# Channel weights prepared in one row behind the first pair's mix, their large transfers issued later

## The reference, cut to what matters

```python
x = x + conv(_ln_c(x))            # relation-aware attention over space, then over channels
t = tokens(x)
t = t + moe(_ln_t(t))             # router over 8 experts, top 2, 128x128 weights per expert
```

```python
theta_c = relu(bn(thc_w @ xc)); phi_c = relu(bn(phc_w @ xc)); g = relu(bn(gxc_w @ xc))   # each (196, 784)
```

## Time and profile before

| | before |
|---|---|
| median of 3 runs | 1772.88 us |
| profiled execution | 1769.24 us |
| its span | 1767.4 us |
| TensorE busy | 1681.3 us (95%) |
| VectorE busy | 1432.0 us (81%) |
| ScalarE busy | 1180.4 us (67%) |
| GpSimd busy | 1110.7 us (63%) |
| mean granted TensorE clock | 0.991 |
| HBM traffic | 106.50 MB read, 26.13 MB written |

### The profile page before, as it was taken

One profiled execution on the slowest core, in us unless ns is written; L12 is line 12 of the kernel. 1 busy time (PEld: TensorE's weight loads), 2 busy tenths in 40 slices (PEclk: granted clock), 3 DMA queues, 4 the chain that ended last, 5 costly groups with the idle time before them and its releaser, 6 DMA issues.

```text
span 1767.4 us, 38965 instructions
## 1 busy us (share of the span) xinstructions
PE 1681.3 (95%) x13140; PEld 1281.1 (72%) x13140; DVE 1432.0 (81%) x4704; ACT 1180.4 (67%) x3346; POOL 1110.7 (63%) x1268
## 2 busy tenths in 40 slices
PE   4789999999999999999999999999999999999985
PEld 3567777777777777777777777777777777777673
DVE  4557888888888888888888888888888888888766
ACT  3557666667766767776676776666677667677543
POOL 1245666676666777666667666666766667675555
PEclk9899999999999999999999999999999999999998
DMA  5122222111222211222221122221112222111110
GB/s 140 37 75 74 76 90 93 71 69 66 93 74 93 93 56 68 81 93 74 93 87 53 65 92 76 91 93 68 72 66 93 74 93 92 56 66 65 56 56 37
DMA packets 56179, 135.15 MB, mean 76 GB/s; under 512 B 16268, under 2 KB 18333, under 8 KB 55982
## 3 DMA queue, kind: packets, MB, share of 16 engines
q1 hardware_dynamic: 55320, 130.81, 21.2%
q10 hardware_dynamic: 662, 1.84, 0.4%
HBM read 106.50 MB, written 26.13 MB: 75 GB/s over the span
## 4 chain that ended last, share of the span: by engine, by line
PE 73%; DVE 13%; ACT 8%; issue 2%; POOL 2%; DMA 1%; SPq 0%; ACTq 0%; POOLq 0%; DVEq 0%
PE low L1246 6%; PE rot L1111 5%; PE rot L1101 5%; PE rot L1102 5%; PE low L1248 5%; PE low L1247 5%; PE high L1246 5%; PE rot L1037 4%; PE high L1248 4%; PE high L1247 4%; ACT part L809 4%; PE rot L1200 3%; PE rot L971 3%; PE rot L981 2%; PE rot L1004 2%; ACT j L703 2%
## 5 line engine op out<-in xcount | busy, mean ns | idle before, releaser
L570 POOL TENSOR_TENSOR part<-part 128x256 f32<-128x256 f32 (+1 forms) x416 | 372.7, 896 | 378.4 <-DVE part L1693 376.1
L809 ACT ACTIVATE part<-low,gv 128x128 f32<-128x128 f32 (+1 forms) x1664 | 468.7, 372 | 149.4 <-PE low L1248 75.6
L1693 DVE SCALAR_TENSOR_TENSOR part<-high,gv,part 128x128 f32<-128x128 f32 x1536 | 421.3, 340 | 22.5 <-ACT part L809 11.5
L575 POOL TENSOR_TENSOR otok<-part 128x128 f32<-128x128 f32 (+1 forms) x416 | 224.9, 541 | 32.6
L1101 PE MATMUL rot<-x1h,wch 128*128 128x256 f32 x960 | 230.7, 281 | 0.0
L1102 PE MATMUL rot<-x1h,wcl 128*128 128x256 f32 x960 | 227.8, 278 | 0.0
L1246 PE MATMUL low<-weh,xh 128*128 128x512 f32 x384 | 174.3, 454 | 18.5 <-ACT part L809 10.9
L753 ACT ACTIVATE chan<-rot,bc 128x256 f32<-128x256 f32 x160 | 68.8, 471 | 172.3 <-PE rot L1113 172.2
L1101 PEld LDWEIGHTS rot<-x1h,wch 128*128 128x128 f32 x960 | 181.0, 189 | 3.2 <-issue 0.3
L1102 PEld LDWEIGHTS rot<-x1h,wcl 128*128 128x128 f32 x960 | 181.0, 189 | 2.6
L1246 PE MATMUL high<-weh,xh 128*128 128x512 f32 x384 | 169.3, 441 | 3.0 <-DVE part L1693 3.0
(11 more groups left out here) (246 smaller groups left out, 3893.3 us busy)
## 6 DMA issues: line engine op xcount, KB each, us to landing
xin<-in_x SPq DMA_DIRECT2D x32, 784.0 KB, 6.1
x<-in_x SPq DMA_DIRECT2D x32, 784.0 KB, 4.3
cen<-shift_rows SPq DMA_DIRECT2D x32, 784.0 KB, 4.1
out<-x SPq DMA_DIRECT2D x64, 392.0 KB, 2.4
y_ch<-rstd_rows SPq DMA_DIRECT2D x32, 768.0 KB, 3.8
otok<-in_ggs_w SPq DMA_DIRECT2D x1, 600.2 KB
tok<-in_ggs_w SPq DMA_DIRECT2D x1, 600.2 KB
rstd_rows<-both_rows SPq DMA_DIRECT2D x32, 7.0 KB
```

What stands on the lines that cost most here:

```text
L570: nc.gpsimd.tensor_tensor(part[0:n, slot, 0:2, :], part[0:n, slot, 0:2, :], part[0:n, slot, 2:4, :], ALU.add).then_inc(sem("half_sum"), 1)
L575: nc.gpsimd.tensor_tensor(otok[0:n, t, :], part[0:n, slot, 0, :], part[0:n, slot, 1, :], ALU.add).then_inc(sem("token_ready"), 1)
L809: last = nc.scalar.activation(part[0:n, turn % RING, e, :], src, ACT.Copy, scale=gv[par(p, back)][0:n, t, e:e + 1])
L1693: last = nc.vector.scalar_tensor_tensor(out=own, in0=src, scalar=gv[par(p, back)][0:n, t, HALF + e:HALF + e + 1], in1=own, op0=ALU.mult, o ...
```

## The change

The seven large transfers are issued by ScalarE behind `space_weights()` instead of in the step ahead. `wide_scales()` moves on VectorE from the end of turn 1 to behind `mix_low(2)` in turn 2, and all of `wide_weights(0)` to `(3)` move on the three engines behind the mix of pair 0 in turn 2, in a row with `(4)`. No instruction is added or removed.

```diff
 # ScalarE
@@ step ahead
                     x_tokens(1, 1, 1)
-                    wide_issue()
                     rstd_copy(1)
@@ turn 2
                 gx(1, 2)
-                if 2 * k + p == 2:
-                    wide_weights(0)
...
                 tp_high(1, 2)
-                if 2 * k + p == 2:
-                    wide_weights(1)
                 tp_tokens(0, 2)
-                if 2 * k + p == 2:
-                    wide_weights(2)
                 tp_tokens(1, 2)
-                if 2 * k + p == 2:
-                    wide_weights(3)
...
                 mix_high(2)
                 if 2 * k + p == 2:
+                    wide_weights(0)
+                    wide_weights(1)
+                    wide_weights(2)
+                    wide_weights(3)
                     wide_weights(4)
@@
             space_weights()
+            wide_issue()
             steps(act, step)
 # TensorE
                 gx(2)
-                if 2 * k + p == 2:
-                    wide_weights(0)
                 finish(0, 5)
...
                 theta_phi(1, 2)
-                if 2 * k + p == 2:
-                    wide_weights(1)
...
                 tp_tokens(0, 2)
-                if 2 * k + p == 2:
-                    wide_weights(2)
                 low_half(11, 5)
                 tp_tokens(1, 2)
-                if 2 * k + p == 2:
-                    wide_weights(3)
...
                 mixed(2)
                 if 2 * k + p == 2:
+                    wide_weights(0)
+                    wide_weights(1)
+                    wide_weights(2)
+                    wide_weights(3)
                     wide_weights(4)
                     late_weights()
 # VectorE
-                if 2 * k + p == 2:
-                    wide_weights(0)
-                    wide_weights(1)
                 residual(1, 1, 4)
...
                 mix_low(2)
                 if 2 * k + p == 2:
+                    wide_scales()
+                    wide_weights(0)
+                    wide_weights(1)
                     wide_weights(2)
                     wide_weights(3)
                     wide_weights(4)
                     late_weights()
...
                 residual(1, 0, 3)
-                if 2 * k + p == 1:
-                    wide_scales()
```

## The result

Over 12 runs each, the changed kernel took 1775.84 us in the median (1771.56 to 1777.87) and the kernel before 1772.25 us (1769.55 to 1775.79). The ratio is 1.0022, 95% interval 1.0014 to 1.0030: slower by some 4 us. The profiled execution has a span of 1772.7 us, 5.3 above that of before.

The account below looks back on a forecast made before the run. TensorE, busy 95% of the span, bounds the kernel, so only the start matters. Gains spent on waiting for xin, issues and the row sum to 58.45 - 57.09 = +1.4 us: 1774.3 us on the median, range 1766.0 to 1777.5.

Parts of the forecast that it names:

- What decides: Start of kernel: turn 2's first joint eviction, before at 57.09 us, settles everything; the rest only shifts with it.
- J: Start of turn 2's first joint product's eviction; 57.09 us before, forecast 58.45.
- (1): Kernel start: large transfers issued later, so small weights land at 15.0 instead of 23.58 us, the row at 18.1 for 24.54.
- (2): ScalarE's seven issues at 24.3 to 27.4 us put gx's eviction at 27.5 instead of a possible 25.9, 1.6 us lost.
- (3): DMA queues: late large transfers on q10 end at 38.4 us and hold up xin, landing at 41.0, bounds 39.3 to 42.
- rival A: Xin is not held up and lands between 32.3 and 34 us; 5.5 to 7.2 us faster, 1766.5; chance 25%.
- (4): Between gx's eviction and x token copies: four interleaved pieces go; TensorE and ScalarE idle about 33 to 41 us instead.
- (5): All five weight groups in a row behind turn 2's mix: 11.3 us from S to the first joint eviction, at 58.45.
- S: Start of the wide scales on VectorE, forecast at T + 6.15 = 47.15 us.
- (6): TensorE's clock: joint products may save 1.9 us, x's transposes and mix may cost up to 2.8; set at 0.
- rival B: Lower clock falls on turn 2's x transposes and mix, S slips 2.8 us: +4.2 us, 1777.1; chance 15%.
- T: Start of the x transposes in turn 2, forecast at 41.0 us.

Follow-up runs that it names:

- e7: Changed kernel with the seven large transfers, uncut, issued by SyncE behind xin in turn 1 instead of by ScalarE; ratio to before 0.9986.
- e11: Changed kernel with the last eight small columns of scales and biases cut to their first 16 elements; ratio to before 1.0002.
- e3: Changed kernel with SyncE issuing xin ahead of its 21 small wide transfers; ratio to before 0.9978.
- e2: Changed kernel with the large transfers issued early as before, so only the row order of the channel weights moves; ratio to before 0.9999.
- e6: Kernel before with only each large transfer cut into a multiple of 16 rows and the rest; ratio to before 0.9979.

## Why the prediction was right, point by point

- **What decides (J, and a one-for-one shift of the rest): right.** Over the 13 kernels of the table the span less J lies between 1708.3 and 1714.0 us, while J itself goes from 51.99 to 64.36. The changed kernel's is 0.8 longer than that of before. The scatter of some 3 us either way goes only in part with TensorE's clock in later stretches: behind J it was at 0.50 for 38 us in the changed kernel and 30 before, but e7, with 32, has a longer rest (1713.2) than e11 with 37 (1711.1).
- **(1) Small weights and the row: right.** 15.18 us for the 15.0 forecast; the row landed at 18.7 for 18.1.
- **(2) ScalarE's issues: right.** gx's eviction at 27.02 for 27.5.
- **(3) xin: right in place, short in size.** 41.0 forecast, 42.7 measured, just outside the upper bound of 42. As counted, nearly all of xin's rows on the four engines came behind q10's end; but q10 ended at 40 and not at 38.4. The sum let it run at its old rate, and from 30 to 34 us, with xin's rows on the other engines, it moved 0.24 MB instead of 0.38, which by the old rate is 1.5 us. The model of strict turns holds for small elements against large rows, and for xin's rows against the weights' in e11, but not in e3 from 28 to 30 us. Its rival A, with xin in by 34, did not occur.
- **(4) The wait in place of the four pieces: right.** TensorE stood idle from 32.1 to 42.8 us, for 33 to 41.
- **(5) The row of five: right.** S to J was 11.40 us for 11.3, and 11.1 to 11.7 in all nine other kernels with the row. It is not what costs: e2.
- **(6) The clock, set at 0: the term that was mis-sized.** The mechanism of rival B occurred at half its price: T to S took 7.42 instead of 6.15, so 1.3 us of the 2.8. The joint products gave 0.6 us back, of the 1.9 allowed: the clock fell there too, but for 3.4 us (60.8 to 64.2) where it had been 6.4, and the first and the last of their evictions were 5.36 us apart instead of 6.00.
- **Sum:** forecast +1.4 us; measured J +4.5, of which xin 1.8 and the clock 1.3 are the two misses, and +3.6 in the medians. The range held, but its width did much of it: it is stretched by rivals A and B. The forecast's own terms allow -2.2 to +2.4 us, which is 1770.7 to 1775.3 and not 1776, and J moved by more than the whole of rival B (+4.2). What happened is the forecast's chain with both of its doubts coming out on the slow side. The mass on "no change" (0.58) was too high for a difference of 0.22%, which lies at the border that I had set.

What the prediction's first part did not draw from its own 24.3% is what e6 shows: the late small weights, which the change cures by moving the large transfers, can be nearly half cured (3.8 of 8.4 us) without moving anything, by cutting those of 68, 60 and 76 rows.

## What to carry to other kernels

```profile
29.03 6.05 SPq L399 DMA_DIRECT2D we<-in_expert_w  x1
35.12 4.29 SPq L399 DMA_DIRECT2D part<-in_expert_b  x1
```

Between two queues, 4-byte elements and 3 KB rows went one to one. Rows of xin and rows of the weights did so in e11 (0.10 MB each from 37 to 39 us), but not in e3 from 28 to 30 us, where by the shares each engine served only one of the two. The Trainium skill, "DMA: Bandwidth & Descriptors", section "Queues, rings and completion order", says that a ring is left only after a whole packet of descriptors, typically 9 to 17. That might go with e3; the earlier trace rows and e11 do not agree with it.
